# A fused grouped convolution and int8-style gated FFN on one core: load order, tile 0, span 31 and the last sums rearranged

## The reference

```
y = conv1d(x, weight, kernel 9, padding 4, groups 4)        # 32 channels in 4 groups of 8
y = y + (cond_128 @ c_weight.T)[:, :, None] + bias          # "shift", one number per (n, channel)
fake_quant(t, axis): s = max(max|t| / 127, 1e-8); round(t / s) * s
qlinear(x, w) = fake_quant(x, -1) @ fake_quant(w, 1).T
gate, up = qlinear(y, w_gate), qlinear(y, w_up)             # 512 -> 1376
out = x + qlinear(silu(gate) * up, w_down)                  # 1376 -> 512
```

## Time and profile before

| what | value |
|---|---|
| median of 3 runs | 295.31 us (295.07 to 295.93) |
| the profiled execution's own time | 295.01 us |
| its span | 293.4 us |
| PE busy | 282.5 us, 96% |
| DVE busy | 251.5 us, 86% |
| POOL busy | 200.8 us, 68% |
| ACT busy | 194.1 us, 66% |
| PE granted clock | printed as 1.00 (2.4 GHz) over the whole span |
| chain of waits | PE 76%, DVE 11%, DMA 4%, POOL 3% |

### The profile page before, as it was taken

How to read it: one execution, slowest core, us unless ns; L and a number is a source line. 1 busy time by engine, 2 the same in 40 slices (tenths; PEclk the granted TensorE clock), 3 DMA queues, 4 the chain that set the end, 5 groups by cost and what they waited for, 6 DMA issues and landing times.

```text
span 293.4 us, 4778 instructions
## 1 busy us (share of the span) xinstructions
PE 282.5 (96%) x1621; PEld 164.4 (56%) x1621; DVE 251.5 (86%) x406; ACT 194.1 (66%) x231; POOL 200.8 (68%) x212
## 2 busy tenths in 40 slices
PE   7998889999999999999999999999999999999994
PEld 7887656654555555555444566655444444444443
DVE  3879789999999997988988878898988889888885
ACT  2259889997777666654778845354788866666640
POOL 1595959998777667653788846552778887666623
PEclk9999999999999999999999999999999999999999
DMA  7999943479967867755389997526355683433345
GB/s 264 413 408 358 412 112 59 106 168 292 208 154 167 189 153 172 204 150 146 102 214 304 221 270 199 156 59 93 104 156 156 159 194 96 87 86 90 101 98 196
DMA packets 83847, 53.36 MB, mean 182 GB/s; under 512 B 69904, under 2 KB 70672, under 8 KB 83696
## 3 DMA queue, kind: packets, MB, share of 16 engines
q1 hardware_dynamic: 83536, 52.89, 67.3%
q10 hardware_dynamic: 288, 0.18, 0.3%
HBM read 27.75 MB, written 8.39 MB: 123 GB/s over the span
## 4 chain that ended last, share of the span: by engine, by line
PE 76%; DVE 11%; DMA 4%; POOL 3%; issue 2%; SPq 2%; ACT 1%; POOLq 1%; DVEq 0%
PE bank L1043 45%; PE bank L1063 21%; PE bank L927 9%; DMA slab<-x_windows 4%; DVE h_max L809 2%; DVE h_mem L803 2%; DVE gu_max L694 2%; DVE y_part L735 1%; SPq L308 1%; SPq L316 1%; POOL h_mem L465 1%; DVE sg_mem L793 1%; DVE y_mem L723 1%; POOL sg_mem L517 1%; POOLq L68 1%
## 5 line engine op out<-in xcount | busy, mean ns | idle before, releaser
L1043 PE MATMUL bank<-wgu_t,xq_mem 128*128 128x512 bf16 (+1 forms) x768 | 155.9, 357 | 1.5 <-DVE h_mem L803 1.0
L517 POOL TENSOR_TENSOR sg_mem<-sg_mem,gu_scale_row 128x512 f32<-128x512 f32 (+1 forms) x96 | 111.3, 1162 | 65.5 <-ACT sg_mem L628 65.5
L1043 PEld LDWEIGHTS bank<-wgu_t,xq_mem 128*128 128x128 bf16 x768 | 73.8, 98 | 73.6 <-DVE h_mem L803 8.4
L628 ACT ACTIVATE sg_mem<-sg_mem,x_scale 128x512 f32<-128x512 f32 (+1 forms) x96 | 63.6, 674 | 44.1 <-DVE sg_mem L793 43.7
L1063 PE MATMUL bank<-wd_t,hq_mem 128*128 128x512 bf16 (+1 forms) x341 | 78.6, 379 | 0.0
L803 DVE SCALAR_TENSOR_TENSOR h_mem<-bank,x_scale,sg_mem 128x512 f32<-128x512 f32 (+1 forms) x96 | 66.4, 692 | 11.8 <-POOL sg_mem L517 10.7
L793 DVE TENSOR_TENSOR sg_mem<-bank,gu_scale_row 128x512 f32<-128x512 f32 (+1 forms) x96 | 60.2, 628 | 14.3 <-PE bank L1043 14.1
L633 ACT ACTIVATE h_mem<-h_mem,h_inv 128x1376 f32<-128x1376 f32 (+1 forms) x32 | 45.3, 1415 | 28.7 <-DVE h_inv L687 28.6
L1063 PEld LDWEIGHTS bank<-wd_t,hq_mem 128*128 128x128 bf16 (+1 forms) x341 | 33.3, 98 | 40.4 <-DMA hq_mem<-hq_mem 0.5
L809 DVE TENSOR_REDUCE h_max<-h_mem 128x1 f32<-128x1376 f32 x32 | 50.5, 1577 | 0.0
L927 PE MATMUL bank<-toeplitz_cut,slab 128*128 128x160 f32 (+1 forms) x320 | 44.8, 291 | 2.4 <-DMA slab<-x_windows 1.8
(11 more groups left out here) (63 smaller groups left out, 136.4 us busy)
## 6 DMA issues: line engine op xcount, KB each, us to landing
slab<-x_windows SPq DMA_DIRECT2D x32, 320.0 KB, 5.0
xo_mem<-x SPq DMA_DIRECT2D x24, 256.0 KB, 3.0
out<-xo_mem SPq DMA_DIRECT2D x24, 256.0 KB, 2.2
hq_mem<-w_gate_up SPq DMA_DIRECT2D x6, 512.0 KB, 6.7
slab<-w_down SPq DMA_DIRECT2D x3, 688.0 KB, 12.5
h_mem<-w_gate_up SPq DMA_DIRECT2D x4, 512.0 KB, 14.1
slab<-x SPq DMA_DIRECT2D x1, 2048.0 KB, 9.1
out<-slab SPq DMA_DIRECT2D x7, 256.0 KB, 2.0
```

What stands on the lines that cost most here:

```text
L517: pool.tensor_tensor(s, s, gu_scale_row[:, 1, at:at + n], ALU.mult).then_inc(silu_scaled, 1)
L628: act.activation(s, s, ACT.Silu, scale=x_scale[:, i:i + 1]).then_inc(silu_done, 1)
L1043: last = pe.matmul(bank[n % 2][:, 0:cols], xq_t[:, g, k, P * c:P * (c + 1)], wgu_t[:, m, k, at:at + cols], start=(k == 0), stop=(k == KT - 1))
```

## The change

1. SP issues the load of span 0 ahead of weight tile 0, and span 1 ahead of weight tile 2.
2. PE runs `conv_span(0)` by itself after 2 empty matmuls, then 14 empty ones, then spans 1 to 3 (before: 22 empty ones, then spans 0 to 3). DVE adds the shift to span 0 before the maximum of weight tile 2.
3. Tile 0. POOL rounds weight tile 10 before its first `scale_silu`, and converts w_down tile 0 after `scale_silu(0, 2)`. ACT copies weight tile 8 before `silu(0, 1)`, and copies span 9 between weight tiles 9 and 10. DVE takes both w_down maxima before `multiply_up(0, 0)`. PE makes the gate piece 2 before it turns the last row of scales.
4. Span 31 is copied by ACT and shifted by POOL, and its fold and the last group's scales move from the end of tile 20 to tile 21, behind the maximum of h.
5. Last sums: tile 30's sum has its own semaphore and does not wait for POOL's earlier sums; tile 31's parts are written to a free `sg_mem` buffer and so don't wait for `down_out` either.

```diff
-        BY_ACT = [2, 3, 4, 5] + list(range(SPANS, 2 * SPANS + 2))
+        BY_ACT = [2, 3, 4, 5] + list(range(SPANS, 2 * SPANS + 2)) + [SLOTS - 1]
-        SPANS_AT = {0: [9, 10], 1: [11], 2: [12, 13], 3: [14, 15]}
+        SPANS_AT = {0: [10], 1: [11], 2: [12, 13], 3: [14, 15]}
-        SHIFTS_AT = {1: [8, 9], 2: [10, 11], 3: [12, 13], 4: [14, 15], 5: [16], 6: [17]}
-        EARLY_FOLDS_AT = {6: [15]}
+        SHIFTS_AT = {1: [8, 9], 2: [10, 11], 3: [12, 13], 4: [14, 15], 5: [16], 6: [17], 20: [31]}
+        EARLY_FOLDS_AT = {6: [15], 21: [31]}
+        FOLDS_AT.pop(20)
...
+            load_span(0)
             load_w(0)
             load_w(1)
-            load_span(0)
+            load_span(1)
             load_w(2)
-            load_span(1)
             load_span(2)
...
             scale_w(JT - 1, 1)
+            round_w(JT - 1)
...
                 scale_silu(i, 0)
-                if i == 0:
-                    round_w(JT - 1)
...
-                for o in down_at(i - 1):
+                for o in down_at(i - 1) if i else []:
                     convert_down(o)
...
                 scale_silu(i, 2)
+                for o in [] if i else down_at(-1):
+                    convert_down(o)
...
             copy_span(8)
+            copy_gate_up(8)
             silu(0, 1)
-            copy_gate_up(8)
             copy_gate_up(9)
+            copy_span(9)
             copy_gate_up(10)
...
                 folds(EARLY_FOLDS_AT.get(i, []))
+                if i == 0:
+                    for o in down_at(0):
+                        weights_down(o)
                 multiply_up(i, 0)
                 if i == 0:
                     multiply_up(i, 1)
-                    for o in down_at(0):
-                        weights_down(o)
...
-                dve.wait_ge(out_ready, i)
                 dve.wait_ge(down_scaled, i + 1)
-                dve.tensor_tensor(xo_of(i), xo_of(i), down_out[:, i % 2, :], ALU.add).then_inc(out_ready, 1)
+                dve.tensor_tensor(xo_of(i), xo_of(i), down_out[:, i % 2, :], ALU.add).then_inc(last_but_one_ready, 1)
...
-                part = down_out[:, i % 2, cols]
-                if half == 0:
-
-                    dve.wait_ge(out_ready, i - 1)
+                part = sg[(i - 1) % SG_BUFS][:, cols]
                 dve.wait_ge(last_down_done, half + 1)
...
-            run_empty(22)
-            for q in range(4):
+            run_empty(2)
+            conv_span(0)
+            run_empty(14)
+            for q in range(1, 4):
                 conv_span(q)
...
                     turn_xq(5)
-                    turn_xq(6)
...
                 gate_or_up(i, 0, 2)
-                if i:
+                if i == 0:
+                    turn_xq(6)
+                else:
                     gate_or_up(i, 1, 1)
```

More of the change, by code:

```diff
@@ L225, in adaln_ffn @@
         last_hq_ready = sem("last_hq_ready")
+        last_but_one_ready = sem("last_but_one_ready")
+        last_ready = sem("last_ready")
         h_rounded = sem("h_rounded")
@@ L356, in store @@
             def store(i):
-                sp.wait_ge(out_ready, i + 1)
+                if i < TILES - 2:
+                    sp.wait_ge(out_ready, i + 1)
+                else:
+                    sp.wait_ge(last_but_one_ready, 1)
                 sp.dma_start(out[:, i, :], xo_of(i))\
@@ L362, in store_last @@
                 cols = slice(HALF * half, HALF * (half + 1))
-                sp.wait_ge(out_ready, TILES + half)
+                sp.wait_ge(last_ready, half + 1)
                 sp.dma_start(out[:, TILES - 1, cols], xo_of(TILES - 1)[:, cols]).then_inc(late_stored, 16)
@@ L756, in _ @@
             weights_inverse(0, 2)
-            weights_top(2)
             dve.wait_ge(shift_ready, 1)
             add_shift(0)
+            weights_top(2)
             add_shift(1)
@@ L903, in finish_last @@
                                          wd_scale_row[:, cols], ALU.mult, ALU.mult).then_inc(last_down_scaled, 1)
-                if half == 0:
-                    dve.wait_ge(out_ready, i)
                 dve.wait_ge(last_down_scaled, half + 1)
-                dve.tensor_tensor(xo_of(i)[:, cols], xo_of(i)[:, cols], part, ALU.add).then_inc(out_ready, 1)
+                dve.tensor_tensor(xo_of(i)[:, cols], xo_of(i)[:, cols], part, ALU.add).then_inc(last_ready, 1)
             for half in range(2):
```

## The result

| | before | after |
|---|---|---|
| median of 12 runs, us | 295.01 | 296.40 |
| lowest to highest, us | 294.90 to 295.93 | 294.65 to 296.85 |
| profiled execution, us (span) | 295.01 (293.4) | 294.65 (293.1) |

The ratio is 1.0032, with an interval from 1.0022 to 1.0043: the changed kernel is slower, by 0.3%. The forecast was 295.2 us and no change that can be told; 296.40 lies 0.1 us above the range.

A forecast was written before the change was run, and what follows sets the result against it. TensorE, busy 96% of the span, was taken as the bound, with four places in its chain of waits touched. Terms -0.1 + 0.3 + 0 - 0.3 = -0.1 us, on the median 295.31, gave 295.2 us; range 294.1 to 296.3.

The forecast's parts named there:

- Tile 0, +0.3 us: Part 3: restart 0.2 us sooner, but channel 2's later transpose starts tile 2 0.5 us later; sum +0.3, ends -0.2 and +0.9.
- clock rival: At the start, TensorE stays slow for longer with fewer empty matmuls and a gap ahead of `conv_span(0)`: 296.8 us, 5%.
- Start, -0.1 us: Parts 1 and 2: engines still wait for span 7's landing at 19.30 us, so 0, taken as -0.1 us.
- hidden by that wait: At the start, the reordered `add_shift(0)` and six empty matmuls less lie ahead of the wait for span 7, costing nothing.
- second rival: At the start, TensorE's quick pace comes later and spans 1 to 3 take twice as long: +1.5, 296.8 us, 5%.
- The transpose of channel 2, a wait of 0.1 to 1.2 us: Ahead of tile 2: issued 1.4 us later, landing taken as 3.0 us after issue, so tile 2 starts 0.5 us later.
- the wait at 46 us: Sign of a right forecast: TensorE waits 0.1 to 1.2 us for a transposing DMA at 46 us.
- The first rival: Ahead of tile 2, channel 2's transpose lands 4.5 to 5 us after issue and becomes the bound: +1.6, 296.9 us, 12%.
- Tile 20, 0: Part 4: `multiply_up(21, 0)` at 207.55 against 207.51, so the stall at 208.32 stays; 0, ends -0.7 and +0.2.
- The end, -0.3 us: Part 5: the last sum no longer waits for GpSimd but for TensorE, starting at 289.8; gain 0.3 us, ends 0 and -0.4.
- The faster case: No wait at tile 2, and either tile 20's stall goes or span 7 is served sooner: -0.9 to -1.2, 294.2 us, 21%.
- Slower: Chance that the kernel is slower, from late channel 2 transpose or slow TensorE at the start: 0.16.

The follow-up runs named there:

- Filling the wait: 24 empty matmuls ahead of TensorE's wait for `multiply_up(1, 0)`, on the kernel before with parts 3, 4 and 5 of the change: 295.51 us, ratio 1.0003.
- The split: Convolution 12 moved from tile 2 into tile 1: with changes 3 to 5 only 295.08 us, on the changed kernel 295.26, there with 12 and 4 empty matmuls too 295.16.
- start alone: Parts 1 and 2 of the change on the kernel before, with the earlier `add_shift(0)`: 295.62 us, ratio 1.0008.
- TensorE's old start: The changed kernel with 22 empty matmuls, then convolutions 0 to 3, as before; the new load order kept: 295.13 us, ratio 1.0005.
- 12 and 4: Empty matmuls around convolution 0 split 12 and 4, not 2 and 14: changed kernel 296.39 us; kernel before with parts 1 and 2 of the change 295.24 us.
- the changed kernel's second series: The changed kernel timed once more without an edit, against the kernel before: 296.05 us, ratio 1.0026.
- the nine without the start: Nine executions not at clock 0.994, of the kernel before with parts 3, 4 and 5 of the change; that run: 294.85 us, ratio 0.9993.
- two variants: Changes 3 to 5 with 24 empty matmuls in the wait, 295.51 us; the changed kernel with convolution 12 moved and 12 and 4 empty matmuls, 295.16 us.
- parts 3 to 5: Parts 3, 4 and 5 of the change on the kernel before, its old load order and start kept: 294.85 us, ratio 0.9993.
- the part alone: Part 4 of the change (tile 20) on the kernel before: 295.37 us, ratio 1.0001.
- By time alone the part: Part 5 of the change (the last sums) on the kernel before: 295.04 us, ratio 0.9995.

## Why the prediction was wrong

**Tile 0, +0.3 us: the step that failed.** The working found where the instructions up to the restart would go, and was right to 0.2 us. The failed sentence is "TensorE restarts at 45.3 instead of 45.51: -0.2". It treats TensorE's wait as empty time of which only the end matters. With nearly the same restart the wait before it had grown from 0.28 to 1.98 us, because TensorE had come to it sooner; and 29 of 72 executions of such kernels had the low mean clock. The one profile that caught it has the fall right behind that wait, at 1.7 us. Filling the wait took the low clock away, on a chip where 13 of 24 executions had it without; that shows the wait as the cause. The split with the restart where it was (45.46) fits, with 0 of 36, but ran on chips 3 and 7, on which no kernel with the wait in one piece ran. The prediction had its clock rival at the start alone, at 5%, and did not ask the same behind any other wait. For an execution that pays it the sum is -0.2 + 1.7 - 0.3 = +1.2, and 295.0 + 1.2 = 296.2, just under where those of the changed kernel lie (296.38 to 296.85). Nor does the -0.2 reach the end: at the last group of matmuls 0.02 us of it were left in the profiled execution. Without it the sum gives 296.4.

The Trainium skill ("TensorE: Matmul & The Clock Gate", "What's actually happening") was cited there for a clock that is low by default and released by activity. What the runs show goes the other way round as well: a clock long at 2.4 GHz was taken back behind one wait, and not in every execution.

**Start, -0.1 us.** Right for the quickest execution, in which TensorE is 0.12 us sooner at its first gate matmuls (28.67 against 28.79), and wrong for most. The failed step is "hidden by that wait": in the two profiles with the long wait for the taps, the restart came 1.12 us (start alone) and 1.35 us (changed kernel) later. TensorE had waited only 0.22 us for span 7 before, and 1.20 us for span 8; these took up its own lateness, but VectorE's went on into tile 0. The mechanism was near the second rival's, with the slow pace on span 0 and the empty matmuls and not on spans 1 to 3, and the price was less than its 1.5: 0.8 us for TensorE's order among the full-clock executions on chip 2, and 0.5 us in the median for the start alone, which the interval can't tell from none. With TensorE's old start, or with 12 and 4, the late executions went away. In the changed kernel's second series the median itself, 296.05, lies among executions at full clock: there the start made it, in the first series the low clock did. In executions at clock 1.0 it is visible: of the thirteen of the changed kernel's two series, eleven took 295.50 to 297.07 and two 294.65 and 295.15, against 294.62 to 295.19 for the nine without the start. In those at 0.994 it hardly is (296.38 to 296.85 with 2 and 14 empty matmuls, 296.21 to 296.82 with 12 and 4). Why the two prices don't add there was not tried.

**The transpose of channel 2, a wait of 0.1 to 1.2 us.** It did not come in the changed kernel's profiles, though its issue was as late as worked out (43.53 in the first): the landing took 2.4 us in both, not the 3.0 that the sum took or the 3.5 of the earlier trace rows. This term was mis-sized, and the wait at 46 us that was to show the forecast right is absent. The reason given for it, that the first ones are slower than all later ones, is wrong too: in the kernel before the 30 transposes of this kind landed 2.3 to 10.6 us after their issue, in the median 2.9. The wait came in two variants, at 0.44 and 0.45 us, by a later issue (44.83 and 44.29) and not by a slow landing (2.4 and 2.6 us). The first rival, its price in full, showed in no profile. Without that wait parts 3 to 5 should have given -0.2 - 0.3 = -0.5; the nine executions at full clock without the start have a median of 294.73 against 295.15, -0.4.

**Tile 20, 0.** Right, in size and reason: `scale_gate(21, 0)` at 201.99 waits for TensorE (202.2 was forecast), `multiply_up(21, 0)` at 207.44 (207.55), and the part alone gave 1.0001.

**The end, -0.3 us.** Right in the trace: 289.74 for the last scaled product (289.8), 0.37 us gained at the last sum. By time alone the part gave 0.9995, within its interval.

**The faster case** came true by half in the profiled execution: no wait for channel 2, and span 7 0.5 us sooner. The stall at 208 us stayed, and 294.65 is not the 294.2 of that case. Slower had too small a chance, since each wait was priced by its end alone.

## What to carry to other kernels

When a change removes small waits of TensorE ahead of a wait that stays, write down the length of the one that is left, not only its end: an idle time that was in pieces and becomes one piece can cost more behind it than the change won. It can be tested in one run, by filling the wait with empty matmuls or moving a piece of other work into it. When work is put off behind a wait that seems to hide it, follow the other engines too: VectorE carried a lateness past TensorE's wait. And look at the clock and time of every execution before trusting the one that was profiled: the profile of the changed kernel was its quickest, and showed a gain.

## What the runs showed of the hardware

- Kernels with one idle stretch of 1.98 us, and 0.67 us idle 7 us before it, had a mean clock of 0.994 in 29 of 72 executions; in the one of these that was profiled, the clock fell to 1.2 GHz behind that stretch, and 16 matmuls took 1.7 us longer. With stretches of 0.71 and 1.22 us it was 0 of 36, with the 1.98 us filled by 1.50 us of matmuls on an identity 0 of 12.
- The fall shows in the granted clock only after TensorE has restarted (1.00 up to 46 us, 0.77 and 0.50 then), so the stretch that pays is not the one that idled.
- In the first 11 us the granted clock is printed as 1.00, while in most profiles a 128-column empty matmul takes 0.12 us and the first convolution of the changed kernel 2.6 to 2.8 us, both about 1.8 times what they take later. When that ends differs from one execution to the next: before 5.5 us in one (22 empty matmuls in 1.39 us), behind 10 us in another (14 in 1.70 us from 8.88 on). The durations tell the pace there, the clock row doesn't.
- The first small loads land 3.1 to 4.6 us (context) and 3.9 to 5.6 us (taps) after their issue from one execution to the next. Placing TensorE's first real work right behind them makes that spread part of the time.
